# The wide product of a low-rank FFN: two parts in reduced fp32, or plain fp32 on two 64-row tiles

## The chip, the cores and the metric

The kernel runs on one core of a Trainium2 chip. The metric is the device time of one execution in microseconds (us); lower is better. The core has a matrix engine (TensorE, PE in the profile; its weight loads are PEld), VectorE (DVE), ScalarE (ACT), GpSimd (POOL) and SyncE (SP), which issues the DMAs. All of them run their own instruction lists and meet at semaphores.

## The reference

Two layers of a gated cross-attention block over x of 16 x 256 tokens x 256 features: a depooling attention and a coupled FFN (layer 0), then an 8-head cross attention and a low-rank FFN (layer 1). Only the last one is touched:

```python
x = x + tanh(g_ffn[1]) * ffn(layernorm(x))
P = x @ U1                 # 256 -> RANK = 64
H = gelu(P @ V1 + b1)      # 64 -> 1024, the wide product
Q = H @ U2                 # 1024 -> 64
y = Q @ V2 + b2            # 64 -> 256
```

## The kernel before, in words

The 4096 tokens lie in SBUF as 32 tiles of 128 tokens. The kernel goes through stages: A and B (layer 0), C (the attention, one batch `b` of 256 tokens per step, 16 steps) and D (the last FFN, `NG` = 8 groups `n` of 512 tokens). Each engine's order is written out by hand, so an engine that waits holds up everything behind it in its own list; PSUM has eight banks, which are reused by name.

Stage D for one group `n`, with the lines of the profile:

- VectorE normalises four token tiles (`xn_d`, L1788). TensorE transposes them (`xnT_d`, L1351) into banks 4 and 5, ScalarE copies them to `d_xnT` (L910).
- TensorE makes the low-rank product P (`lowrank_d`, L1361). `u1_sb` has 64 columns, and the 512 tokens are cut into two halves of 256: half 0 goes to PSUM partitions 0 to 63 of bank 4, half 1 to partitions 64 to 127. Two feature chunks `c` are summed, so there are four matmuls in plain fp32. VectorE copies each half to `d_pT` as fp32r (L1799: the high part) and writes the rest, value less high part, to the other 64 partitions (L1803: the low part). So `d_pT` holds 64 ranks high and 64 ranks low for all 512 tokens.
- TensorE makes the wide product in four steps `j` of two 128-column tiles `e` (`hidden_d(n, j)`). `v1_sb` holds V1 twice, on partitions 0 to 63 and 64 to 127, and GpSimd has split it once, in stage C, into `v1_hi` and `v1_lo` (`split_v1`, L664 and L666). For each tile a matmul with `v1_hi` (L1439) and one with `v1_lo` (L1440) sum over all 128 rows into one bank: four fp32r matmuls of 512 columns for each `j`.
- ScalarE takes Gelu of two banks (L972) into `d_h`. TensorE makes Q (`second_d(n, j)`, L1449: two column tiles of 64), VectorE copies it (L1870), TensorE makes y (`out_d`, L1462: two row tiles of 64 rows, in banks 7 and 5), VectorE adds it to x (L1877), GpSimd has added b2 before (L680), SyncE stores the group.

The order on TensorE around the change is in `body_d(n)`: hidden 0, hidden 1, transposes of group n+2, second 0, hidden 2, second 1, hidden 3, low-rank product of group n+2, out of group n-1, second 2, second 3. The low-rank products of groups 0 and 1 are made in the last step of stage C (`body_c`), the first two hidden steps of group 0 stand before that stage's last output product (L1325). On VectorE `body_d(n)` is: `xn_d(n + 2)`, `lowrank_d(n + 2)`, `out_d(n - 1)`, `second_d(n)` (the copy of Q).

In the profile a plain fp32 matmul is two records, so "x8" of L1361 is four matmuls; an fp32r matmul is one record. Stage B has one product of the shape used below, `layer4_b` (L1092): weights and data on 64 rows, two tiles `u` on rows 0 to 63 and 64 to 127, 512 columns, plain fp32, banks 0 and 1.

Of the kernel before, what the change touches and what calls it, by code (L numbers as in the profile page):

```python
# [18 lines left out]
F32 = mybir.dt.float32  # L19
F32R = mybir.dt.float32r  # L20
I32 = mybir.dt.int32
BF16 = mybir.dt.bfloat16
ALU = mybir.AluOpType
# [3 lines left out]
P = 128  # L27
# [3 lines left out]
DK = D // P  # L31
FK = DC // P
GROUP = 512
GT = GROUP // P
HALF = GROUP // 2
NG = B * S // GROUP
HEADS, HD = 8, 32
QH = 4
F = 1024
RANK = 64  # L40
# [23 lines left out]
LEAD = 2  # L64
KB = 1024
# [50 lines left out]
def need(eng, sem, count):  # L116

    if isinstance(count, int) and count <= 0:
        return
    eng.wait_ge(sem, count)  # L120
# [22 lines left out]
def beyond(b, n):  # L143
    return isinstance(b, int) and b >= n


def is_last(b, n):
    return isinstance(b, int) and b == n - 1


def is_at(b, n):
    return isinstance(b, int) and b == n


def is_first(b):
    return isinstance(b, int) and b == 0


def build(nc, x, ctx_in, lens, mask, g_xattn, g_ffn, w_in, b_in, g_res, g_init,
# [7 lines left out]
    with ExitStack() as whole:  # L167
        def sb(name, shape, dt=F32, stack=whole):
            return stack.enter_context(nc.sbuf_tensor(name, shape, dt))

        def sem(name):
            return whole.enter_context(nc.semaphore(name))

        banks = whole.enter_context(nc.psum_tensor("bank", [P, 8, 512], F32))
        bank = [banks[:, i, :] for i in range(8)]
# [24 lines left out]
        bk_col = sb("bk_col", [P, DK])  # L200
        bq_col = sb("bq_col", [P, DK])
        neg_row = sb("neg_row", [B, S])
        u1_sb = sb("u1_sb", [P, DK, RANK])
        v1_sb = sb("v1_sb", [P, F // P, P])
        b1_col = sb("b1_col", [P, F // P])
        u2_sb = sb("u2_sb", [P, F // P, RANK])
# [109 lines left out]
            c_sum = [sb(f"c_sum{h}", [P, TS, QH], F32, st) for h in range(2)]  # L316
            c_inv = [sb(f"c_inv{h}", [P, TS, QH], F32, st) for h in range(2)]
        with ExitStack() as st:
            v1_hi = sb("v1_hi", [P, F // P, P], F32R, st)
            v1_lo = sb("v1_lo", [P, F // P, P], F32R, st)  # L320
            d_xn = [sb(f"d_xn{s}", [P, GT, D], F32, st) for s in range(2)]
            d_pT = [sb("d_pT0", [P, GROUP], F32R, st)]
            sb("c_last", [P, 72 * KB // 4], F32, st)
            d_xnT = [sb(f"d_xnT{s}", [P, DK, GROUP], F32, st) for s in range(2)]
            d_h = [sb(f"d_h{s}", [P, 2, GROUP], F32, st) for s in range(2)]
            d_pT += [sb(f"d_pT{s}", [P, GROUP], F32R, st) for s in range(1, LEAD)]
            d_qT = [sb(f"d_qT{s}", [P, HALF], F32, st) for s in range(2)]


        s_lens, s_wa, s_wb, s_wc, s_wd = (sem(n) for n in ("lens_in", "weights_a_in", "weights_b_in",  # L330
                                                           "weights_c_in", "weights_d_in"))
# [28 lines left out]
        b_back, b_x2 = sem("b_result_in_psum"), sem("b_x_updated")  # L360
# [16 lines left out]
        c_nbn, c_nstat, c_npre, c_next = (sem("c_" + n) for n in (  # L377
            "next_bn", "next_moments", "next_chain", "next_stats_ready"))

        s_v1, d_phi = sem("v1_parts_ready"), sem("d_lowrank_high_ready")  # L380
        d_xn_ok, d_xT_ps, d_xT_ok, d_p_ps, d_p_ok, d_h_ps, d_h_ok = (sem("d_" + n) for n in (
            "xn_ready", "xnT_in_psum", "xnT_copied", "lowrank_in_psum", "lowrank_copied",
            "hidden_in_psum", "hidden_ready"))
# [7 lines left out]
        def row_on_all(v):  # L391
# [28 lines left out]
            (arange[:], row_on_all(adaptive_range)),  # L420
        ]
        loads_d = [
            (u1_sb[:], u1.rearrange("(c p) r -> p c r", p=P)),
            (v1_sb[0:RANK], v1.rearrange("r (c f) -> r c f", f=P)),
            (v1_sb[RANK:2 * RANK], v1.rearrange("r (c f) -> r c f", f=P)),
            (b1_col[:], column(b1)), (u2_sb[:], u2.rearrange("(c p) r -> p c r", p=P)),
# [14 lines left out]
        def scores_free(eng, b, hg):  # L441

            n = QH // 2 * (2 * b + hg)
            need(eng, c_pT_act, n)
            need(eng, c_pT_dve, n)
# [83 lines left out]
        def _(pool):  # L529
# [84 lines left out]
            def stats_b(n):  # L614
                next_stats(n, n % 2, GT, b_mv[n % 2], b_tmp[n % 2], b_nstat, b_npre, b_next, n + 1)
# [4 lines left out]
            def bias_c(b):  # L620
                need(pool, c_xn_ok, b + 1)
                xb = x_sb[:, bass.ds(TS * b, TS), :]
                nc.gpsimd.tensor_tensor(xb, xb, bout_b[:].unsqueeze(1).to_broadcast([P, TS, D]),
                                        ALU.add).then_inc(c_xb, 1)
# [9 lines left out]
            def split_q(b):  # L634
                need(pool, c_qhi_ok, b + 1)
                nc.gpsimd.tensor_tensor(c_parts[:, Q_LO, :, :], c_qT[:], c_parts[:, Q_HI, :, :].bitcast(F32),  # L636
                                        ALU.subtract).then_inc(c_qlo_ok, 1)

            def ones_c(s, before, count):
                pool.wait_ge(before, count)  # L640
                nc.gpsimd.memset(c_stack[s][MASK_ROW:MASK_ROW + 1, 0, :, :, :].bitcast(F32), 1.0).then_inc(s_ones, 1)
                pool.wait_ge(s_ones, s + 1)

            def body_c(b, s):
                if not is_last(b, B):
                    split_q(b + 1)
                    bias_c(b + 1)
                if is_first(b):
                    pool.wait_ge(c_xb, 2)
                    ones_c(1, b_x2, NG)  # L650
                if not is_first(b):
                    next_stats(b - 1, 1 - s, TS, n_mv[1 - s], n_tmp[1 - s], c_nstat, c_npre, c_next, b)
                if not beyond(b + 2, B):
                    split_k(b + 2)
                if isinstance(b, int) and b < 2:
                    stats_b(NG // 2 + 2 * b)
                    stats_b(NG // 2 + 2 * b + 1)
                if is_at(b, 1):
                    split_v1()

            def split_v1():
                pool.wait_ge(s_wd, 16 * len(loads_d))
                pool.wait_ge(b_x2, NG)
                nc.gpsimd.tensor_copy(v1_hi[:], v1_sb[:]).then_inc(s_v1, 1)  # L664
                pool.wait_ge(s_v1, 1)
                nc.gpsimd.tensor_tensor(v1_lo[:], v1_sb[:], v1_hi[:].bitcast(F32), ALU.subtract).then_inc(s_v1, 1)  # L666

            split_q(0)
            ones_c(0, c_qlo_ok, 1)
# [320 lines left out]
        def _(pe):  # L990
            mm = nc.tensor.matmul
# [3 lines left out]
            for k in range(TS):  # L995
                op = nc.tensor.transpose(bank[6][:, k * B:(k + 1) * B], bound[:, k * P:(k + 1) * P],
                                         ident[0:B, 0:B])
# [3 lines left out]
            for b in range(B):  # L1001
                for k in range(TS):
                    op = mm(bank[0][0:HI, b * LO:(b + 1) * LO], hit_hi[:, k * B + b, :], hit_lo[:, k * B + b, :],
                            start=k == 0, stop=k == TS - 1)
# [3 lines left out]
            for c in range(DK):  # L1008
                for o in range(DK):
                    op = nc.tensor.transpose(bank[5][:, c * D + o * P:c * D + (o + 1) * P],  # L1010
                                             win_raw[:, o, c * P:(c + 1) * P], ident[:])
# [151 lines left out]
            for lo in range(LO):  # L1163
                op = nc.tensor.transpose(bank[1][0:B, lo:S:LO], ends[:, :, lo], ident[0:HI, 0:HI])
# [190 lines left out]
            def lowrank_d(n):  # L1355
                if n == 0:
                    pe.wait_ge(s_wd, 16 * len(loads_d))
                need(pe, d_xT_ok, 2 * n + 2)
                for c in range(DK):
                    for half in range(2):  # L1360
                        op = mm(bank[4][half * RANK:(half + 1) * RANK, 0:HALF], u1_sb[:, c, :],  # L1361
                                d_xnT[n % 2][:, c, half * HALF:(half + 1) * HALF], start=c == 0, stop=c == DK - 1)
                op.then_inc(d_p_ps, 1)

            def body_c(b, s):
# [31 lines left out]
                if last:  # L1397
                    lowrank_d(1)
# [19 lines left out]
            for k in range(TS):  # L1418
                for f in range(FK):
                    op = mm(bank[3][:, k * D:(k + 1) * D], c_ctxT[0][:, f, k * P:(k + 1) * P],  # L1420
                            wsrcT[:, f, D:2 * D], start=f == 0, stop=f == FK - 1)
# [13 lines left out]
            def hidden_d(n, j):  # L1435
                need(pe, d_p_ok, n + 1)
                need(pe, d_h_ok, 4 * n + j - 1)
                for e in range(2):
                    mm(bank[2 * (j % 2) + e][:], v1_hi[:, 2 * j + e, :], d_pT[n % LEAD][:], start=True, stop=False)  # L1439
                    op = mm(bank[2 * (j % 2) + e][:], v1_lo[:, 2 * j + e, :], d_pT[n % LEAD][:],  # L1440
                            start=False, stop=True)
                op.then_inc(d_h_ps, 1)

            def second_d(n, j):
# [36 lines left out]
                second_d(n, 2)  # L1481
                second_d(n, 3)

            pe.wait_ge(s_v1, 2)
            scores_free(pe, B, 0)
            hidden_d(0, 0)
            hidden_d(0, 1)
# [7 lines left out]
        def _(dve):  # L1495
            v = nc.vector
# [295 lines left out]
            def lowrank_d(n):  # L1792
                need(dve, d_p_ps, n + 1)
                need(dve, d_h_ps, 4 * (n - LEAD + 1))
                parts = [slice(half * RANK, (half + 1) * RANK) for half in range(2)]
                tokens = [slice(half * HALF, (half + 1) * HALF) for half in range(2)]
                pT = d_pT[n % LEAD]
                for half in range(2):
                    op = v.tensor_copy(pT[parts[half], tokens[half]], bank[4][parts[half], 0:HALF])  # L1799
                op.then_inc(d_phi, 1)  # L1800
                need(dve, d_phi, n + 1)
                for half in range(2):
                    op = v.tensor_tensor(pT[parts[1 - half], tokens[half]], bank[4][parts[half], 0:HALF],  # L1803
                                         pT[parts[half], tokens[half]].bitcast(F32), ALU.subtract)
                op.then_inc(d_p_ok, 1)

            def body_c(b, s):
# [110 lines left out]
```

## Time and profile before

| | before |
|---|---|
| median of 3 runs | 746.27 us (742.38, 746.27, 746.42) |
| profiled execution: its own time | 746.62 us |
| profiled execution: span of the trace | 744.8 us |
| PE busy | 687.0 us (92%) |
| DVE, ACT, POOL busy | 513.4, 417.7, 207.5 us |
| stage D with its lead-in, 648 us to the end | 97 us |

The span is what the trace covers; the execution's own time is 1.8 us longer. All times of rows are from the span's start.

### The profile page before, as it was taken

How to read it: one execution, taken by the hardware profiler on the slowest of the kernel's cores; microseconds unless marked ns; L12 is line 12 of the kernel's file. 1: busy time of each engine (PE TensorE's matmuls, PEld its weight loads, DVE VectorE, ACT ScalarE, POOL GpSimd, SP SyncE). 2: the span in 40 equal slices, each digit the busy share in tenths (PEclk: the TensorE clock that was granted, in tenths of full speed). 3: DMA queues.
4: the chain of work that ended last, by engine and by line, in shares of the span. 5: the costliest groups of instructions: out<-in, count | busy, mean ns of one | idle time of the engine just before them, and what ended most of it. 6: DMA issues, size and time to landing. Idle time of an engine off the chain costs nothing.

```text
span 744.8 us, 12430 instructions
## 1 busy us (share of the span) xinstructions
PE 687.0 (92%) x3874; PEld 484.1 (65%) x3874; DVE 513.4 (69%) x976; ACT 417.7 (56%) x1119; POOL 207.5 (28%) x278
## 2 busy tenths in 40 slices
PE   2959999999999999698999999999999997999996
PEld 1646555554544458586888888888888886656553
DVE  6675477755766458879878778878778888735422
ACT  3666645536555534474755665665666567555452
POOL 5454433310110032146132223313232321052110
PEclk9979999999999999799999999999999999999999
DMA  7821103910000004431344432344433223001012
GB/s 199 258 85 57 57 29 105 237 60 1 1 0 1 0 1 113 114 89 50 92 114 113 113 75 73 80 111 113 113 88 87 77 60 86 1 1 57 29 57 86
DMA packets 45752, 57.46 MB, mean 77 GB/s; under 512 B 13808, under 2 KB 24208, under 8 KB 45584
## 3 DMA queue, kind: packets, MB, share of 16 engines
q1 hardware_dynamic: 45712, 56.97, 28.5%
q8 instruction: 20, 0.33, 0.2%
q14 instruction: 20, 0.16, 0.1%
HBM read 27.46 MB, written 4.19 MB: 42 GB/s over the span
## 4 chain that ended last, share of the span: by engine, by line
PE 73%; ACT 9%; DVE 8%; issue 3%; SPq 3%; DMA 2%; POOL 1%; ACTq 0%; DVEq 0%; POOLq 0%
PE bank L1066 11%; PE bank L1325 7%; ACT c_p L882 7%; PE bank L1252 6%; PE bank L1304 6%; PE bank L1078 5%; PE bank L1449 4%; PE bank L1318 4%; PE bank L1291 4%; PE bank L1270 4%; PE bank L1042 4%; DVE c_nmx L1754 3%; PE bank L1046 3%; PE bank L1439 2%; SPq L500 2%
## 5 line engine op out<-in xcount | busy, mean ns | idle before, releaser
L882 ACT ACTIVATE c_p<-bank,c_nmx 128x256 f32<-128x256 f32 x256 | 117.5, 488 | 34.9 <-DVE c_nmx L1754 34.9
L1767 DVE TENSOR_TENSOR c_p<-c_p,c_inv 128x1024 f32<-128x1024 f32 x64 | 90.1, 1409 | 1.1
L1066 PE MATMUL bank<-b_o,cw 128*128 128x512 f32 x192 | 90.8, 603 | 0.0
L1754 DVE TENSOR_REDUCE c_nmx<-bank 128x4 f32<-128x1024 f32 x64 | 75.4, 1219 | 19.1 <-PE bank L1291 19.1
L1304 PE MATMUL bank<-ident,c_p 128*128 128x128 f32 x512 | 66.9, 280 | 13.1 <-ACT c_p L882 13.1
L1304 PEld LDWEIGHTS bank<-ident,c_p 128*128 128x128 f32 x512 | 59.2, 144 | 21.6 <-ACT c_p L882 12.3
L738 ACT ACTIVATE b_h<-bank,cb 128x512 f32<-128x512 f32 x48 | 33.0, 687 | 55.9 <-PE bank L1066 55.9
L1252 PE MATMUL bank<-c_ctxT,wsrcT 128*128 128x256 f32 x256 | 62.2, 388 | 1.4 <-ACT c_ctxT L858 1.4
L972 ACT ACTIVATE d_h<-bank,b_col 128x512 f32<-128x512 f32 x64 | 39.6, 686 | 39.6 <-PE bank L1440 39.6
L1066 PEld LDWEIGHTS bank<-b_o,cw 128*128 128x128 f32 x192 | 34.2, 190 | 41.6 <-issue 41.2
L1774 DVE COPY c_pT<-bank 128x512 f32<-128x512 f32 x64 | 44.0, 687 | 21.7 <-PE bank L1304 21.7
L1270 PE MATMUL bank<-wsrcT,c_ctxT 128*128 128x256 f32 x240 | 56.7, 379 | 0.0
L882 ACT ACTIVATION_READ_ACCUMULATOR c_p<-bank,c_nmx 128x1 f32 x256 | 56.3, 220 | 0.0
L636 POOL TENSOR_TENSOR c_parts<-c_qT,c_parts 128x512 fp32r<-128x512 f32 x16 | 20.6, 1290 | 124.9 <-ACT c_parts L864 124.9
L1252 PEld LDWEIGHTS bank<-c_ctxT,wsrcT 128*128 128x128 f32 x256 | 48.4, 194 | 8.1 <-ACT c_ctxT L858 1.9
L1270 PEld LDWEIGHTS bank<-wsrcT,c_ctxT 128*128 128x128 f32 x240 | 45.5, 190 | 6.2
L892 ACT COPY c_pT<-bank 128x512 f32<-128x512 f32 x64 | 38.0, 599 | 11.1 <-PE bank L1304 11.1
L1629 DVE TENSOR_SCALAR b_tt<-b_tt,k_tt,b_kb 128x256 f32<-128x256 f32 x48 | 17.7, 410 | 37.6 <-ACT b_tt L754 37.6
L1078 PE MATMUL bank<-b_h,cw 128*128 128x512 f32 x96 | 43.3, 592 | 0.0
L1291 PEld LDWEIGHTS bank<-c_stack 97*128 97x128 f32 x256 | 32.8, 191 | 15.7 <-issue 12.1
L1291 PE MATMUL bank<-c_stack 97*128 97x256 f32 x256 | 39.5, 298 | 3.0 <-DMA c_stack<-neg_row 3.0
L897 ACT COPY c_upT<-bank 128x256 f32<-128x256 f32 x32 | 11.9, 373 | 53.9 <-PE bank L1318 53.9
(188 smaller groups left out, 1390.2 us busy)
## 6 DMA issues: line engine op xcount, KB each, us to landing
c_stack<-c_parts SPq DMA_DIRECT2D x192, 128.0 KB
a_ctx<-in_ctx SPq DMA_DIRECT2D x16, 512.0 KB, 3.6
c_ctx<-in_ctx SPq DMA_DIRECT2D x16, 512.0 KB, 3.4
out_x<-x_sb SPq DMA_DIRECT2D x8, 512.0 KB, 3.0
x_sb<-in_x SPq DMA_DIRECT2D x3, 1024.0 KB, 9.9
mask_b<-in_mask_BxS_fk SPq DMA_DIRECT2D x1, 2048.0 KB, 12.4
x_sb<-in_x SPq DMA_DIRECT2D x2, 512.0 KB, 7.5
wsrc_raw<-in_L_xattn_W_src SPq DMA_DIRECT2D x1, 1024.0 KB, 6.9
```

What stands on the lines that cost most here:

```text
L882: op = nc.scalar.activation(c_p[hg][:, tc, j, :], scores(tc)[:, j, :], ACT.Exp, bias=c_nmx[hg][:, tc, j:j + 1], accum_out=c_sum[hg][:, tc, ...
L972: op = nc.scalar.activation(d_h[j % 2][:, e, :], bank[2 * (j % 2) + e][:], ACT.Gelu_apprx_tanh, bias=b1_col[:, 2 * j + e:2 * j + e + 1])
L1066: op = mm(bank[2 * u + h][:], cw1[:, c, h * P:(h + 1) * P], b_o[n % LANES][:, c, :], start=c == 0, stop=c == DK - 1)
L1078: op = mm(bank[4 + u][:], cw2[:, c, :], b_h1[u][:, c, :], start=i == 0, stop=i == DK - 1)
L1252: op = mm(bank[dst][:, m * S:(m + 1) * S], wsrcT[:, f, m * P:(m + 1) * P], c_ctxT[s][:, f, :], start=f == 0, stop=f == FK - 1)
L1270: op = mm(bank[4][:, k * D:(k + 1) * D], c_ctxT[s][:, f, k * P:(k + 1) * P], wsrcT[:, f, D:2 * D], start=f == 0, stop=f == FK - 1)
L1291: op = mm(scores(tc)[:, j, :], c_stack[s][:, 0, j, hg, tc * P:(tc + 1) * P], c_stack[s][:, 1, j, hg, :], start=True, stop=True)
L1304: op = nc.tensor.transpose(bank[j][:, q * S + tc * P:q * S + (tc + 1) * P], c_p[hg][:, tc, j, q * P:(q + 1) * P], ident[:])
L1325: return mm(bank[7][:, k * D:(k + 1) * D], src[:, k * P:(k + 1) * P], woutT[:, f, :], start=f == 0, stop=f == 2 * DK - 1)
L1754: v.tensor_reduce(c_nmx[hg][:, tc, :], scores(tc), AXIS.X, ALU.max, negate=True)\
L1767: v.tensor_tensor(pr, pr, c_inv[hg][:, :, js].unsqueeze(3).to_broadcast([P, TS, 2, S]), ALU.mult)\
L1774: v.tensor_copy(c_pT[hg][:, j, :], bank[j][:]).then_inc(c_pT_dve, 1)
```

## The change

V1 is no longer split: the wide product takes `v1_sb` and P as they are, in plain fp32. For that P has to stand on partitions 0 to 63 and again on 64 to 127, for all 512 tokens. This is done in the low-rank product: `u1_sb` holds U1 twice side by side (128 columns, one more load), and two matmuls of 512 tokens and 128 columns take the place of four of 256 tokens and 64 columns. VectorE then makes one copy of the whole bank. In `hidden_d` tile e = 0 is computed on rows 0 to 63 and tile e = 1 on rows 64 to 127, each with one fp32 matmul. `split_v1` and both semaphores of the parts go; a placeholder keeps the memory of what follows in its place.

```diff
-        u1_sb = sb("u1_sb", [P, DK, RANK])
+        u1_sb = sb("u1_sb", [P, DK, 2 * RANK])
...
-            v1_hi = sb("v1_hi", [P, F // P, P], F32R, st)
-            v1_lo = sb("v1_lo", [P, F // P, P], F32R, st)
+            sb("b_last", [P, 8 * KB // 4], F32, st)
-            d_pT = [sb("d_pT0", [P, GROUP], F32R, st)]
+            d_pT = [sb("d_pT0", [P, GROUP], F32, st)]
...
-            (u1_sb[:], u1.rearrange("(c p) r -> p c r", p=P)),
+            (u1_sb[:, :, 0:RANK], u1.rearrange("(c p) r -> p c r", p=P)),
+            (u1_sb[:, :, RANK:2 * RANK], u1.rearrange("(c p) r -> p c r", p=P)),
...
-                if is_at(b, 1):
-                    split_v1()
...
                 for c in range(DK):
-                    for half in range(2):
-                        op = mm(bank[4][half * RANK:(half + 1) * RANK, 0:HALF], u1_sb[:, c, :],
-                                d_xnT[n % 2][:, c, half * HALF:(half + 1) * HALF], start=c == 0, stop=c == DK - 1)
+                    op = mm(bank[4][:], u1_sb[:, c, :], d_xnT[n % 2][:, c, :], start=c == 0, stop=c == DK - 1)
                 op.then_inc(d_p_ps, 1)
...
                 for e in range(2):
-                    mm(bank[2 * (j % 2) + e][:], v1_hi[:, 2 * j + e, :], d_pT[n % LEAD][:], start=True, stop=False)
-                    op = mm(bank[2 * (j % 2) + e][:], v1_lo[:, 2 * j + e, :], d_pT[n % LEAD][:],
-                            start=False, stop=True)
+                    rows = slice(e * RANK, (e + 1) * RANK)
+                    op = mm(bank[2 * (j % 2) + e][:], v1_sb[rows, 2 * j + e, :], d_pT[n % LEAD][rows, :],
+                            start=True, stop=True)
                 op.then_inc(d_h_ps, 1)
...
-            pe.wait_ge(s_v1, 2)
             scores_free(pe, B, 0)
...
             def lowrank_d(n):
                 need(dve, d_p_ps, n + 1)
                 need(dve, d_h_ps, 4 * (n - LEAD + 1))
-                parts = [slice(half * RANK, (half + 1) * RANK) for half in range(2)]
-                tokens = [slice(half * HALF, (half + 1) * HALF) for half in range(2)]
-                pT = d_pT[n % LEAD]
-                for half in range(2):
-                    op = v.tensor_copy(pT[parts[half], tokens[half]], bank[4][parts[half], 0:HALF])
-                op.then_inc(d_phi, 1)
-                need(dve, d_phi, n + 1)
-                for half in range(2):
-                    op = v.tensor_tensor(pT[parts[1 - half], tokens[half]], bank[4][parts[half], 0:HALF],
-                                         pT[parts[half], tokens[half]].bitcast(F32), ALU.subtract)
+                op = v.tensor_copy(d_pT[n % LEAD][:], bank[4][:])
                 op.then_inc(d_p_ok, 1)
```

## Rows read from the trace of the kernel before

**Rows 1.** The page: busy time of each engine; shares of the chain that ended last.

```profile
PE 687.0 (92%) x3874; PEld 484.1 (65%) x3874; DVE 513.4 (69%) x976; ACT 417.7 (56%) x1119; POOL 207.5 (28%) x278
...
PE 73%; ACT 9%; DVE 8%; issue 3%; SPq 3%; DMA 2%; POOL 1%; ACTq 0%; DVEq 0%; POOLq 0%
```

**Rows 2.** Timeline (start, length, engine, line, count), PE, one group of stage D.

```profile
695.81 0.50 PE L1439 MATMUL bank<-d_pT,v_hi 128*128 128x512 f32 x1
...
697.86 1.09 PE L1351 MATMUL bank<-ident,d_xn 128*128 128x128 f32 x8
698.88 1.08 PE L1449 MATMUL bank<-d_h,u_sb 128*64 128x256 f32 x8
699.90 0.50 PE L1439 MATMUL bank<-d_pT,v_hi 128*128 128x512 f32 x1
...
701.03 1.08 PE L1449 MATMUL bank<-d_h,u_sb 128*64 128x256 f32 x8
...
703.17 1.08 PE L1361 MATMUL bank<-d_xnT,u_sb 128*64 128x256 f32 x8
...
704.18 1.14 PE L1462 MATMUL bank<-v_sb,d_qT 64*128 64x256 f32 x8
...
705.25 1.95 PE L1449 MATMUL bank<-d_h,u_sb 128*64 128x256 f32 x16
...
707.13 0.50 PE L1439 MATMUL bank<-d_pT,v_hi 128*128 128x512 f32 x1
```

**Rows 3.** Timeline, DVE, the same group.

```profile
696.10 0.41 DVE L1870 COPY d_qT<-bank 128x256 f32<-128x256 f32 x1
...
696.43 1.38 DVE L1788 TENSOR_SCALAR d_xn<-x_sb,mu,rstd 128x256 f32<-128x256 f32 x4
...
704.30 0.86 DVE L1799 CAST d_pT<-bank 64x256 fp32r<-64x256 f32 x2 [6.50 <-PE bank L1361]
```

**Rows 4.** Timeline, PE, stage B around one row-tiled product in plain fp32.

```profile
96.59 1.13 PE L1092 MATMUL bank<-b_h,cw 64*128 64x512 f32 x4
...
97.65 1.98 PE L1066 MATMUL bank<-b_o,cw 128*128 128x512 f32 x4
...
99.47 0.60 PE L1029 MATMUL bank<-ident,a_xs 128*128 128x128 f32 x4
```

**Rows 5.** Timeline of PE from 277.60 to 277.75 us: what is under way then.

```profile
277.69 0.70 PE L1092 MATMUL bank<-b_h,cw 64*128 64x512 f32 x2
```

**Rows 6.** Windows: us, busy PE, PEld, DVE, ACT, POOL (x), PE clock, DMA, GB/s.

```profile
718.43:728.22 9.79, 9.36 (x59) 5.48 (x57) 2.10 (x4) 4.96 (x8) 0.00 (x0) 1.00 0.16 54
```

**Rows 7.** Timeline, last step of stage C.

```profile
629.44 1.06 PE L1304 MATMUL bank<-ident,c_p 128*128 128x128 f32 x8 [1.63 <-ACT c_p L882]
...
638.30 1.08 PE L1361 MATMUL bank<-d_xnT,u_sb 128*64 128x256 f32 x8
...
640.44 0.69 DVE L1774 COPY c_pT<-bank 128x512 f32<-128x512 f32 x1 [0.22 <-PE bank L1304]
...
643.21 1.07 PE L1318 MATMUL bank<-c_pT,c_v 128*32 128x256 f32 x16 [1.57 <-issue]
```

**Rows 8.** Timeline, groups 0 and 1 of stage D.

```profile
655.66 7.09 POOL L680 TENSOR_TENSOR x_sb<-x_sb,b_b 128x1024 f32<-128x1024 f32 x3
...
661.16 2.72 DVE L1788 TENSOR_SCALAR d_xn<-x_sb,mu,rstd 128x256 f32<-128x256 f32 x4
...
663.93 1.09 PE L1351 MATMUL bank<-ident,d_xn 128*128 128x128 f32 x8 [1.29 <-DVE d_xn L1788]
```

**Rows 9.** Timeline, PE, group 6: the product behind its first Gelu.

```profile
720.99 1.08 PE L1449 MATMUL bank<-d_h,u_sb 128*64 128x256 f32 x8 [0.43 <-ACT d_h L972]
```

**Rows 10.** Timeline, stage C, batch 2: the split of V1 and what stands beside it.

```profile
344.07 2.36 POOL L666 TENSOR_TENSOR v_lo<-v_sb,v_hi 128x1024 fp32r<-128x1024 f32 x1
...
344.66 2.24 DVE L1727 TENSOR_SCALAR c_xn<-x_sb,mu,rstd 128x256 f32 x2
...
346.76 1.97 PE L1304 MATMUL bank<-ident,c_p 128*128 128x128 f32 x8 [0.57 <-ACT c_p L882]
```

More of the change, by code:

```diff
@@ L325, in build @@
             d_h = [sb(f"d_h{s}", [P, 2, GROUP], F32, st) for s in range(2)]
-            d_pT += [sb(f"d_pT{s}", [P, GROUP], F32R, st) for s in range(1, LEAD)]
+            d_pT += [sb(f"d_pT{s}", [P, GROUP], F32, st) for s in range(1, LEAD)]
             d_qT = [sb(f"d_qT{s}", [P, HALF], F32, st) for s in range(2)]
@@ L378, in build @@
             "next_bn", "next_moments", "next_chain", "next_stats_ready"))
-        s_v1, d_phi = sem("v1_parts_ready"), sem("d_lowrank_high_ready")
         d_xn_ok, d_xT_ps, d_xT_ok, d_p_ps, d_p_ok, d_h_ps, d_h_ok = (sem("d_" + n) for n in (
@@ L657, in body_c @@
                     stats_b(NG // 2 + 2 * b + 1)
-                if is_at(b, 1):
-                    split_v1()
[L661 to L666, printed above, removed]
             split_q(0)
```

## The prediction

> **What bounds the kernel now.** The page first: PE is busy 92% of the span and holds 73% of the chain that ended last [rows 1]. An average says nothing of the last stage, so the timeline of one of its groups comes next [rows 2]: from 695.81 to 707.13 us, 11.32 us for group 3, PE goes from product to product with no gap over 0.1 us. Stage D is bound by PE's own list. Two places are not: the transposes of a later group may wait for VectorE (below), and in groups 6 and 7, which have no transposes to fill in, PE waits for Gelu [rows 9]; such a group takes 9.79 us with PE busy for 9.36, at the full granted clock, 1.00, which is 2.4 GHz [rows 6].
>
> **Streaming and switches.** An isolated hidden step, four fp32r records, takes 1.13 us to the next product (699.90 to 701.03), two steps in a row 2.05 (695.81 to 697.86) [rows 2]. So four further records cost 0.92, 0.23 each, and 0.21 goes at the borders. Those borders are changes of the tile shape: after one, four plain fp32 records of 128 rows and 512 columns take 1.82 us (97.65 to 99.47) [rows 4]; a plain fp32 record of that size is twice one fp32r record less overhead, about 0.43, four are 1.72, and 0.10 is the tail of the switch. The rest of the 0.21 stands ahead of the first record.
>
> **Part 1, the wide product.** The new step is two matmuls on 64 rows, 512 columns, plain fp32: four records. This very form is in stage B: L1092 takes 1.06 us from its start to the next product (96.59 to 97.65) [rows 4], with two records under way at once [rows 5]; in a row they would need 4 x 0.43 = 1.72. So an isolated step goes from 1.13 to 1.06, a gain of 0.07, not the half that the count of matmuls (16 to 8 for each group) suggests. The pair in a row goes from 2.05 to 1.06 + 0.86 = 1.92, and then comes a switch to the transposes that was not there, 0.10 ahead of them and 0.10 after their first record.
> The Trainium skill, "TensorEngine Tiling (Array Packing)", Key Properties, speaks against the change here: going to another tiling mode, not just another tile, drains the engine. The trace agrees with its 0.2 us for each switch. By that rule alone each of six groups pays 0.2 more, in full.
> By the rows part of it is covered. From 695.81 to 697.86 VectorE also runs a chain: it copies Q at 696.10, normalises from 696.43 for 1.38 to 697.81, and the transposes start 0.05 later [rows 2, 3]. The chain starts when Q's last product is out, and the change leaves it alone, so the transposes start 2.05 after the hidden step as before. I charge only the 0.10 after their first record, between 0 (the switch is done while PE waits) and 0.20.
>
> **Part 2, the low-rank product.** Now 1.01 us to the next product (703.17 to 704.18) [rows 2], two column tiles at a time. After: four records of 128 x 128, 512 columns, behind a switch, 1.82 [rows 4], and 0.09 to the row-tiled out product, 1.91: +0.90 for each of groups 0 to 5. In group 0 no out product stands between it and second 2; a switch more, +0.10.
> For low-rank product 1, at the end of stage C, both neighbours are 128 x 128, so it takes 1.72 and starts 0.10 earlier than at 638.30: the next product is 0.61 later. Is that on the path? VectorE waited for that next product, 0.22 us, at 640.44, and the work behind its copy releases the product at 643.21 [rows 7]. So yes: +0.61, bounds 0 and 0.90. Low-rank product 0 costs nothing: behind it PE waits 1.63 us for ScalarE's exponentials [rows 7]; without that cover it would be 0.9 too.
>
> **Part 3, VectorE.** Four operations of 64 x 256, two in 0.86 us [rows 3] and as much again for the two subtractions, give way to one 128 x 512 copy from PSUM, 0.69 [rows 7]: 1.1 us less for each group. It is worth nothing in steady groups: P for group n+2 is used a group later. Behind it on VectorE stand `out_d`, the copy of Q and the normalising. The copy begins 0.9 later than now, ends 0.2 earlier, and two additions follow before second 3 is out; none of this is late.
>
> **Part 4, GpSimd and the load.** The split goes: 2.36 us for the low part [rows 10] and less for the high one. Beside it VectorE's two normalisings take 2.24 us where four take 1.38 [rows 3, 10]. But PE's next transposes at 346.76 are released by ScalarE's exponentials, not by VectorE [rows 10]: I take 0; bounds: a gain up to 1.5, a loss of 0. The second load of U1 is one issue more on SP, ahead of its wait for the end of stage A; SP's next loads stand behind that wait, and U1 is used only at the end of stage C. I take 0; without that cover it is the length of one issue, well under 1 us.
>
> **The sum, from the first shift on.**
> - End of stage C: +0.61. Group 0: hidden 0 and 1 +0.07 (a switch more before the output product), hidden 2 and 3 -0.14, low-rank +1.00: +0.93. Together +1.54.
> - Group 1's transposes at 663.93 waited 1.29 us for VectorE. Its normalising took 2.72 where 1.38 is usual, from 661.16 on; three GpSimd operations ran until 655.66 + 7.09 = 662.75 [rows 3, 8]. It looks as if the first of the four had to wait for GpSimd; from 662.75 to its end are 1.14. GpSimd comes only 0.68 later (0.61 + 0.07), VectorE could start 1.54 later, at 662.70, still before 663.43: the transposes come 0.68 later. The wait swallows the rest; what is left is +0.68. Bounds: 0.1 and the full 1.6.
> - Rest of group 1: -0.14 + 0.90 = +0.76. Groups 2 to 5: 4 x 0.76 = +3.04. The tail of the new switch in groups 1 to 5: 5 x 0.10 = +0.50.
> - Groups 6 and 7: no low-rank product; three pieces of hidden work on the path, 2 x 3 x -0.07 = -0.42 (the wait for Gelu stays, and starts a little earlier).
> Sum: 0.68 + 0.76 + 3.04 + 0.50 - 0.42 = +4.56 us. The span goes to 749.4, the profiled execution's own time from 746.62 to 751.2. That execution is 0.35 above the median of the runs, 746.27, so the median becomes 750.8, 0.6% more. With all low bounds the sum is 2.0 (3.5, less 1.5 from stage C), with all high ones 6.3 (another 0.3 from stage C, 0.92 without the wait, 0.5 of switches).
>
> **The rivals.**
> - The row tiles do not overlap (slower). Place: every hidden step; each takes 1.72 + 0.2 in place of 1.06, or 0.86 more, 32 steps: +27.5, 778 us. It decides as soon as a tenth of it comes true. For it: weights of both tiles come from one tensor. Against: L1092 is the same form and overlaps [rows 4, 5]. 0.03.
> - A new wait (slower). VectorE has a cushion of some 0.6 us between its second addition and the copy of Q; if the later low-rank copy eats it, the copy of Q, the normalising and the transposes slide. Each microsecond per group is 5 us; at 0.7 per group the time is 754.5. For it: 2.05 was already VectorE's chain. Against: the new copy is shorter. 0.08.
> - The gains elsewhere cancel the loss (same). If taking the split away frees the attention step of batch 2, and group 1's wait takes all, 747 us. 0.09.
> - The wide product halves (faster): if the two tiles ran with records as short as fp32r's 0.23, a step would take 0.67, 0.4 less in 32 steps: 738 us. Against: L1092's 1.06. 0.02. The Trainium skill, "TensorEngine Tiling (Array Packing)", Theoretical Speedup, gives up to twofold for a contraction of 64; the trace shows that, but against plain fp32, not against the fp32r records of now.
> - The forecast, 0.78: a loss of 2.0 to 6.3 us.
>
> **The numbers.** Predicted 750.8. One of the three runs before was 3.9 below the others, so a median may fall low: the range is 746.5 to 754.5, and leaves out what lies beyond the bounds and the first and last rival. What a measurement of this kernel can tell from no change is 1%, 7.5 us: below 738.8 or above 753.7. Faster 0.02; slower 0.10 (the serial tiles, most of the new wait); same 0.88.
>
> **What the profile after would show.** Hidden steps of 1.06 us alone and transposes 2.05 after a pair's start: right; 1.7 or more: serial tiles. The low-rank product 1.9 us to the next. A steady group of about 12.2 in place of 11.32 us. Group 1's transposes near 664.6. Stage C before 638 unmoved; a shift there is what I have priced at nothing. If the transposes are released by VectorE more than 2.1 after the pair's start, it is the new wait.

## The result and the profile after

| | before | after |
|---|---|---|
| median | 746.01 us (742.38 to 748.39, 13 runs) | 748.69 us (747.08 to 750.99, 13 runs) |
| ratio, with 95% interval | | 1.0041 [1.0025, 1.0057] |
| profiled execution: its span | 744.8 us | 746.8 us |
| PE / DVE / ACT / POOL busy | 687.0 / 513.4 / 417.7 / 207.5 us | 687.5 / 505.3 / 417.5 / 204.1 us |

By the ratio the change costs 3.1 us (1.9 to 4.3); the two medians lie 2.7 apart. That is within the 1% that I called no change, clear of zero, and the time is inside the range of 746.5 to 754.5. 750.8 was predicted, 2.1 too much. The engines' busy times say where not to look: VectorE and GpSimd work less than before [rows 1], and the kernel is slower all the same.

The start of an execution scatters: the kernel after, e3, e4 and e5 have the same instructions up to stage D, and they reach the first product of attention probabilities and values of stage C (L1308) between 307.5 and 310.5 us. From 352 us on, the two traces keep their distance through all of stage C (the same product comes at 351.95 before and 351.16 after, and the transposes of its last step at 629.44 and 628.65, both times 0.79 earlier). So I compare stretches from the end of stage C on. First a steady group after, in the timeline of PE (start, length, engine, line, count); the wide product is now L1428, the low-rank product L1350, the transposes L1341, second L1437, out L1450:

```profile
697.59 1.99 PE L1428 MATMUL bank<-d_pT,v_sb 64*128 64x512 f32 x8
...
699.50 1.09 PE L1341 MATMUL bank<-ident,d_xn 128*128 128x128 f32 x8
700.53 1.08 PE L1437 MATMUL bank<-d_h,u_sb 128*64 128x256 f32 x8
...
701.54 1.13 PE L1428 MATMUL bank<-d_pT,v_sb 64*128 64x512 f32 x4
702.60 1.08 PE L1437 MATMUL bank<-d_h,u_sb 128*64 128x256 f32 x8
...
703.61 1.13 PE L1428 MATMUL bank<-d_pT,v_sb 64*128 64x512 f32 x4
704.67 1.98 PE L1350 MATMUL bank<-d_xnT,u_sb 128*128 128x512 f32 x4
...
706.59 1.13 PE L1450 MATMUL bank<-v_sb,d_qT 64*128 64x256 f32 x8
...
707.65 1.95 PE L1437 MATMUL bank<-d_h,u_sb 128*64 128x256 f32 x16
...
709.53 1.99 PE L1428 MATMUL bank<-d_pT,v_sb 64*128 64x512 f32 x8
```

Read it from start to start, against [rows 2]. The group takes 11.94 us instead of 11.32. A hidden step alone takes 1.06 to 1.07 (701.54 to 702.60), not 1.13. The low-rank product takes 1.92 (704.67 to 706.59), not 1.01. And the two hidden steps in a row take 1.91 to the transposes (697.59 to 699.50), where the prediction kept the 2.05 of before. The reason is on VectorE, in the same stretch:

```profile
697.70 0.42 DVE L1848 COPY d_qT<-bank 128x256 f32<-128x256 f32 x1 [0.47 <-PE bank L1437]
...
698.04 1.37 DVE L1775 TENSOR_SCALAR d_xn<-x_sb,mu,rstd 128x256 f32<-128x256 f32 x4
...
706.70 0.69 DVE L1782 COPY d_pT<-bank 128x512 f32<-128x512 f32 x1 [7.28 <-PE bank L1350]
...
707.77 1.41 DVE L1855 SCALAR_TENSOR_TENSOR x_sb<-bank,gates,x_sb 128x512 f32<-128x512 f32 x2 [0.38 <-PE bank L1450]
```

The copy of Q starts 0.11 us behind the hidden step's start and has waited for PE. Before, it started 0.29 behind (696.10 against 695.81) [rows 2, 3], without any wait: VectorE still had its additions to finish, which had stood behind four low-rank operations. The additions of that group in the timeline before:

```profile
694.77 1.41 DVE L1877 SCALAR_TENSOR_TENSOR x_sb<-bank,gates,x_sb 128x512 f32<-128x512 f32 x2
696.10 0.41 DVE L1870 COPY d_qT<-bank 128x256 f32<-128x256 f32 x1
```

Where the first extra time arises, and how much of it group 1's wait takes back (timeline after: low-rank product 1 on PE, VectorE's copy of c_pT behind it, the product that waits for that copy's successors, then PE and VectorE in group 1):

```profile
637.42 1.88 PE L1350 MATMUL bank<-d_xnT,u_sb 128*128 128x512 f32 x4
...
640.21 0.69 DVE L1761 COPY c_pT<-bank 128x512 f32<-128x512 f32 x1 [0.77 <-PE bank L1294]
...
642.97 1.07 PE L1308 MATMUL bank<-c_pT,c_v 128*32 128x256 f32 x16 [1.93 <-issue]
...
661.28 1.99 PE L1428 MATMUL bank<-d_pT,v_sb 64*128 64x512 f32 x8
...
661.74 1.88 DVE L1775 TENSOR_SCALAR d_xn<-x_sb,mu,rstd 128x256 f32<-128x256 f32 x4
...
663.68 1.09 PE L1341 MATMUL bank<-ident,d_xn 128*128 128x128 f32 x8 [0.40 <-DVE d_xn L1775]
```

VectorE now waits 0.77 us for PE at the end of stage C where it waited 0.22 [rows 7]: 0.55 more, straight onto the path. PE waits 0.40 us for VectorE in group 1 where it waited 1.29 [rows 8].

The books of the two traces, each stretch from a product's start to another's, in us. "Update product" is the product of attention probabilities and values (L1318 before, L1308 after), the last one before stage D; "tail" is the prediction's charge for the new switch:

| stretch | before | after | difference | predicted |
|---|---|---|---|---|
| end of stage C: 629.44 to 643.21; 628.65 to 642.97 | 13.77 | 14.32 | +0.55 | +0.61 |
| group 0: last update product to group 1's first hidden step | 13.52 | 14.51 | +0.99 | +0.93 |
| group 1: that step to its transposes | 3.40 | 2.40 | -1.00 | -0.86 |
| rest of group 1 | 9.27 | 10.02 | +0.75 | +0.76, +0.10 tail |
| groups 2 to 5 | 45.23 | 47.77 | +2.54 | +3.04, +0.40 tails |
| groups 6 and 7, to the last out product | 20.16 | 19.37 | -0.79 | -0.42 |
| sum | | | +3.04 | +4.56 |

The sum of the stretches, 3.04, agrees with the 3.1 of the timed runs. It is 1.52 under the predicted sum, and the misses hardly cancel: 0.90 of the 1.52 lies in groups 2 to 5, 0.37 in groups 6 and 7.

### The profile page after: what moved, and what is told of

It is laid out like the page before. It is cut to its first block, busy times and chain, and to the rows that moved or that the text cites. A ratio compares the mean times of both kernels' runs of the same rounds, so it can differ in the third digit from the quotient of the medians.

```text
span 746.8 us, 12339 instructions
## 1 busy us (share of the span) xinstructions
PE 687.5 (92%) x3842; PEld 471.2 (63%) x3842; DVE 505.3 (68%) x952; ACT 417.5 (56%) x1119; POOL 204.1 (27%) x276
## 4 chain that ended last, share of the span: by engine, by line
PE 73%; DVE 9%; ACT 9%; issue 3%; SPq 3%; DMA 2%; POOL 1%; ACTq 0%; DVEq 0%; POOLq 0%
PE bank L1056 11%; PE bank L1315 7%; ACT c_p L872 6%; PE bank L1242 6%; PE bank L1294 6%; PE bank L1068 5%; PE bank L1437 4%; PE bank L1308 4%; PE bank L1428 4%; PE bank L1260 4%; PE bank L1281 4%; PE bank L1032 3%; DVE c_nmx L1741 3%; PE bank L1036 2%; SPq L499 2%
## 5 line engine op out<-in xcount | busy, mean ns | idle before, releaser
L1294 PE MATMUL bank<-ident,c_p 128*128 128x128 f32 x512 | 65.4, 277 | 12.7 <-ACT c_p L872 12.7
```

What stands on the lines that cost most here:

```text
L1294: op = nc.tensor.transpose(bank[j][:, q * S + tc * P:q * S + (tc + 1) * P], c_p[hg][:, tc, j, q * P:(q + 1) * P], ident[:])
```

## The experiments

Theory A, from the prediction and the traces: the doubled low-rank product is the whole loss; the wide product, at the same rate as before, gives a little back; what VectorE has in its list ahead of its copy of Q also counts. Each of the rivals is in the texts below. Times of kernels are against the kernel before in the same runs, whose median was 745.5 us for the first four and 745.4 for the last four.

### One part alone: the doubled low-rank product (e1)

```diff
 # before.py with the doubled u1_sb and its two matmuls, and in VectorE's lowrank_d:
+                pT, low = d_pT[n % LEAD], slice(RANK, 2 * RANK)
+                v.tensor_copy(pT[:], bank[4][:]).then_inc(d_phi, 1)
+                need(dve, d_phi, n + 1)
+                op = v.tensor_tensor(pT[low, :], bank[4][low, :], pT[low, :].bitcast(F32), ALU.subtract)
```

> Only the low-rank product is doubled (128 columns, 512 tokens); the wide product stays on the high and low parts in fp32r, VectorE makes one 128x512 copy and one 64x512 subtraction. Theory A (the whole loss is the doubled low-rank product, the wide product gives a little back): low-rank product to the out product 1.8 us instead of 1.01, a steady group 11.9 to 12.0 us instead of 11.32, the time about 3.5 to 4 us over the kernel before, that is at least as much as with the full change. Rival B (the loss is the wide product in plain fp32, with its changes of tile shape): most of the loss is gone, within 1 us of the kernel before.

Measured: 748.56 us, ratio 1.0040 [1.0024, 1.0055], the same as with the full change; that is 3.0 us over the kernel before, a little less than the 3.5 to 4 expected. In the timeline of PE, the ends of one steady group and its low-rank product (L1361; L1461 is out):

```profile
697.63 0.50 PE L1438 MATMUL bank<-d_pT,v_hi 128*128 128x512 f32 x1
...
699.58 1.04 PE L1352 MATMUL bank<-ident,d_xn 128*128 128x128 f32 x8
700.55 1.08 PE L1448 MATMUL bank<-d_h,u_sb 128*64 128x256 f32 x8
...
704.74 1.88 PE L1361 MATMUL bank<-d_xnT,u_sb 128*128 128x512 f32 x4
...
706.55 1.14 PE L1461 MATMUL bank<-v_sb,d_qT 64*128 64x256 f32 x8
...
709.49 0.50 PE L1438 MATMUL bank<-d_pT,v_hi 128*128 128x512 f32 x1
```

1.81 us for the low-rank product and 11.86 for the group. The loss of the full change is there without its wide product; rival B falls. The lines show one thing more: the hidden steps are those of before, but VectorE has two operations of P instead of four, and the pair takes 1.95 to the transposes (L1352) instead of 2.05, these 0.97 to second 0 instead of 1.02.

### The other part alone: the wide product (e2)

```diff
 # after.py with u1_sb, its load and lowrank_d of TensorE as before; VectorE:
-                op = v.tensor_copy(d_pT[n % LEAD][:], bank[4][:])
+                for half in range(2):
+                    src = slice(half * RANK, (half + 1) * RANK)
+                    for dst in (src, slice((1 - half) * RANK, (2 - half) * RANK)):
+                        op = v.tensor_copy(d_pT[n % LEAD][dst, half * HALF:(half + 1) * HALF], bank[4][src, 0:HALF])
```

> Only the wide product is changed (plain fp32 on two 64-row tiles); the low-rank product stays as two column tiles of 64, and VectorE makes four 64x256 copies so that P stands on both halves of the partitions. Theory A: hidden steps 1.06 us, the pair to the transposes 2.05 because VectorE still has four operations ahead of its chain, a steady group 11.19 us, groups 6 and 7 about 9.4 instead of 9.79; 1.5 us under the kernel before. Rival B: slower than the kernel before by 2 to 3 us. Rival C (VectorE's queue does not matter, TensorE alone sets the group): the pair to the transposes is 1.92 here too, a steady group 11.05.

Measured: 743.20 us, ratio 0.9976 [0.9964, 0.9988]: by the ratio 1.8 us faster than before (0.9 to 2.7). Timeline, PE and VectorE, one group:

```profile
694.40 1.99 PE L1429 MATMUL bank<-d_pT,v_sb 64*128 64x512 f32 x8
694.67 0.41 DVE L1852 COPY d_qT<-bank 128x256 f32<-128x256 f32 x1
...
696.43 1.09 PE L1340 MATMUL bank<-ident,d_xn 128*128 128x128 f32 x8
...
702.73 1.73 DVE L1786 COPY d_pT<-bank 64x256 f32<-64x256 f32 x4 [6.36 <-PE bank L1350]
...
705.55 1.99 PE L1429 MATMUL bank<-d_pT,v_sb 64*128 64x512 f32 x8
```

The group takes 11.15 us. The pair to the transposes takes 2.03, although the hidden steps are those of the changed kernel: with four operations back in VectorE's list the copy of Q starts 0.27 late again. Rival C, under which it would be 1.92, falls.

### No second row tile (e3)

```diff
-                    rows = slice(e * RANK, (e + 1) * RANK)
+                    rows = slice(0, RANK)
```

> The changed kernel with both 128-column tiles of a hidden step computed on rows 0 to 63, so that no two matmuls stand on different row tiles. Theory A (the two row tiles work at the same time, each record takes 0.43 us): a hidden step takes 1.72 + 0.2 = 1.9 us instead of 1.06, 32 steps, about +27 us, 775 us. Rival D (a record of 64 rows is simply half as long, whatever the tile): a hidden step stays at 1.06, 749 us.

Measured, one execution: 775.62 us, span 772.9. A hidden step in the timeline of PE, and the product behind it:

```profile
701.43 1.98 PE L1428 MATMUL bank<-d_pT,v_sb 64*128 64x512 f32 x4
703.34 1.08 PE L1437 MATMUL bank<-d_h,u_sb 128*64 128x256 f32 x8
```

1.91 us in place of 1.06. So a plain fp32 record of 512 columns takes 0.43 us on 64 rows as on 128 (1.91 less 0.2 at the borders, by four), rival D falls, and the 1.06 comes from two of them at a time. This is the price of the first rival of the prediction, had it come true: 27 us.

### More work on VectorE (e4)

```diff
                 op = v.tensor_copy(d_pT[n % LEAD][:], bank[4][:])
+                for i in range(4):
+                    rows = slice(i % 2 * RANK, (i % 2 + 1) * RANK)
+                    op = v.tensor_copy(d_junk[rows, i * HALF:(i + 1) * HALF], bank[4][rows, 0:HALF])
```

> The changed kernel with four more 64x256 copies (4 x 0.43 = 1.72 us) on VectorE behind the copy of P, into memory that nothing reads. Theory A (VectorE's list has some 0.85 us to spare between the copy of P and the copy of Q; what goes over it is paid in the wait of the transposes): the pair of hidden steps to the transposes 2.75 to 2.8 us instead of 1.91, a steady group 12.8 instead of 11.94, 752 us. The step as the prediction put it (VectorE's operations here are worth nothing in steady groups): 11.94, 749 us.

Measured, one execution: 750.19 us, 2 under the 752 expected. Timeline of one group:

```profile
697.67 1.99 PE L1428 MATMUL bank<-d_pT,v_sb 64*128 64x512 f32 x8
698.52 0.41 DVE L1851 COPY d_qT<-bank 128x256 f32<-128x256 f32 x1
...
700.28 1.09 PE L1341 MATMUL bank<-ident,d_xn 128*128 128x128 f32 x8 [0.62 <-DVE d_xn L1775]
...
710.30 1.99 PE L1428 MATMUL bank<-d_pT,v_sb 64*128 64x512 f32 x8
```

A group of 12.63 us, the pair to the transposes 2.61: 0.70 more for 1.72 more work, so 1.0 us of VectorE's work is free here, not the 0.85 of theory A. Groups 2 to 5 make 2.8 us of it in the trace; the single execution shows 1.5 over the median of the kernel after, within the scatter of the start. That VectorE's work is worth nothing is refuted by the transposes' wait, not by the whole time.

### GpSimd out of VectorE's way (e5)

```diff
-            def bias_d(n, s):
-                need(pool, d_xn_ok, n + 1)
+            def bias_d(n):
+                need(pool, d_xn_ok, n + 2 if n == LEAD else n + 1)
...
-            over_pairs(pool, NG, bias_d)
+            for n in range(NG):
+                bias_d(n)
```

> The changed kernel; GpSimd's bias addition for group 2 waits until VectorE has normalised group 3, so GpSimd is idle while VectorE normalises group 3. Theory A (the wait of group 1's transposes is VectorE's first normalising operation held up by GpSimd's running addition): the four operations take 1.38 us instead of 1.88, the transposes come about 1.92 us after the pair of hidden steps' start, set by TensorE's own list, instead of 2.40; half a microsecond less, 748.2 us. Rival (it is the copy of Q or the semaphores' latency that make them late): 2.40 stays.

Measured, one execution: 747.79 us; 748.2 was expected, and a single time cannot tell it from the 748.7 of the kernel after. Timeline, groups 0 and 1:

```profile
655.11 4.67 POOL L670 TENSOR_TENSOR x_sb<-x_sb,b_b 128x1024 f32<-128x1024 f32 x2
...
660.89 1.99 PE L1429 MATMUL bank<-d_pT,v_sb 64*128 64x512 f32 x8
...
661.35 1.37 DVE L1776 TENSOR_SCALAR d_xn<-x_sb,mu,rstd 128x256 f32<-128x256 f32 x4
...
662.81 1.09 PE L1342 MATMUL bank<-ident,d_xn 128*128 128x128 f32 x8
```

With GpSimd idle the four operations take 1.37 us instead of 1.88, and the transposes come 1.92 behind the pair's start instead of 2.40. The wait in group 1, which swallowed a microsecond of the change's cost, was GpSimd's addition in front of VectorE; the rival, by which 2.40 stays, falls.

### Toward a faster kernel (e6, e7, e8)

e6 is e2 with the four copies moved to ScalarE, behind its last Gelu of a group:

```diff
 # ScalarE, for n >= LEAD; VectorE's lowrank_d returns there
+            def lowrank_d(n):
+                need(act, d_p_ps, n + 1)
+                need(act, d_h_ps, 4 * (n - LEAD + 1))
+                (the four copies of e2, with nc.scalar.copy)
+                op.then_inc(d_p_ok, 1)
```

> As e2 (only the wide product changed, the low-rank product in two column tiles of 64), but for groups 2 to 7 ScalarE makes the four copies of P, after its last Gelu of the group, and VectorE makes none. Theory A (in e2 VectorE's four copies push its copy of Q back by 0.15 us): the pair to the transposes 1.92 us instead of 2.03, a steady group 11.03 instead of 11.15, ScalarE still done with the copies before its next Gelu; some 0.5 us under e2, 742.7 us. Rival E (ScalarE's queue becomes the wait): the next Gelu starts late and a steady group is 11.3 or more.

e7 adds the diff of e5:

> e6 with the later bias addition of e5. Theory A: group 1's transposes, which in e2 came 3.43 us after the pair's start, come 2.0 to 2.1 us after it; 1.4 us under e6, 741.3 us, 0.6% under the kernel before. Rival: the wait stays, because another operation of VectorE is late.

e8 is e7 with, in `body_d` of TensorE:

```diff
+                if n + LEAD < NG:
+                    need(pe, d_xT_ok, 2 * (n + LEAD) + 2)
+                if n > 0:
+                    out_d(n - 1, 1 - n % 2)
                 if n + LEAD < NG:
                     lowrank_d(n + LEAD)
-                if n > 0:
-                    out_d(n - 1, 1 - n % 2)
```

> e7 with the out product of the group before moved ahead of the low-rank product, so that it follows the hidden step in the same tile shape (64 rows) and the low-rank product stands beside second 2 in the same shape (64 columns). Theory A (0.1 us ahead of and 0.1 behind each change of tile shape, which these two moves save): hidden 3 to out 0.96 us, out to low-rank product 1.06, low-rank product to second 2 0.92; a steady group 10.85 us, five groups, about 1 us under e7, 740.4 us. Rival (the shape costs nothing, the 0.2 is the latency of a semaphore wait at the head of each product): as e7.

| kernel | time | ratio to before, 95% interval | steady group | stage D |
|---|---|---|---|---|
| before | 745.4 to 746.0 | 1 | 11.32 | 91.6 |
| after | 748.69 | 1.0041 [1.0025, 1.0057] | 11.94 | 94.1 |
| e2 | 743.20 | 0.9976 [0.9964, 0.9988] | 11.15 | 90.0 |
| e6 | 744.57 | 0.9991 [0.9974, 1.0008] | 11.04 | 89.6 |
| e7 | 742.39 | 0.9966 [0.9950, 0.9981] | 11.04 | 88.2 |
| e8 | 741.71 | 0.9948 [0.9928, 0.9968] | 10.69 | 86.4 |

"Stage D" is the distance in the trace from the last update product of stage C to the last out product. By it e6 is 0.44 us under e2, as expected, and e7 1.4 under e6. The whole times of e6 do not show it: 742.7 was expected, and its median is 1.4 over e2's, with an interval that holds 1. The profiled execution of e6 loses its time before stage D, which it enters 2.5 us later than e2's (below). In e7 group 1's transposes come 2.02 us behind the pair's start, where e2 has 3.43. Rival E falls too: ScalarE's four copies take 1.49 us and it is idle for 2.37 behind them.

e8 gained more than expected in a group, 0.35 instead of 0.2. Its timeline of PE:

```profile
707.84 1.13 PE L1441 MATMUL bank<-d_pT,v_sb 64*128 64x512 f32 x4
708.90 1.08 PE L1450 MATMUL bank<-d_h,u_sb 128*64 128x256 f32 x8
709.91 1.13 PE L1441 MATMUL bank<-d_pT,v_sb 64*128 64x512 f32 x4
710.88 1.03 PE L1463 MATMUL bank<-v_sb,d_qT 64*128 64x256 f32 x8
711.84 1.08 PE L1362 MATMUL bank<-d_xnT,u_sb 128*64 128x256 f32 x8
712.75 1.90 PE L1450 MATMUL bank<-d_h,u_sb 128*64 128x256 f32 x16
714.58 1.99 PE L1441 MATMUL bank<-d_pT,v_sb 64*128 64x512 f32 x8
```

The same hidden step costs 1.06 us before a product of another shape (707.84) and 0.97 before out, which has its own shape (709.91). Out costs 0.96 instead of 1.07, the low-rank product 0.91 instead of 1.01. The rival, a wait's latency at each product's head, would have left them as they were; e8 even has a wait more ahead of out. It has the lowest median of the kernels run, by the ratio 3.9 us under the one before (2.4 to 5.4). It is not shown to be faster than e7: the two intervals overlap, the medians are 0.7 apart where stage D says 1.8, and e8's profiled execution enters stage D 2.1 us later than e7's. Both stayed above what was expected, 741.3 for e7 and 740.4 for e8.

## Why the prediction was right, and where it was off

**The wide product** was right: 1.06 us alone, because the trace of before had the very form. Halving the matmuls was never worth half the time: one fp32r record is 0.23 us, one plain fp32 record 0.43, and the two row tiles just make up for the difference (e3).

**The low-rank product** was right, and it is the loss: 1.92 us measured, 1.91 predicted. e1 has the whole loss, e2 has none of it. Low-rank product 0, in the gap of stage C, was free, as said: PE still waits behind it, 1.19 us instead of 1.63 [rows 7].

**The end of stage C** was right in place and size, +0.55 against +0.61.

**"It is worth nothing in steady groups" was wrong.** The prediction saw that VectorE's chain to the transposes set 2.05 us, but let it start "when Q's last product is out", and gave VectorE "a cushion of some 0.6 us" ahead of the copy of Q. The trace of before has no such cushion: the additions run until 696.18, and the copy starts at 696.10. It started 0.29 us after the hidden step instead of 0.11, since it stood behind the additions, and those behind four low-rank operations. One copy in place of four operations takes VectorE off the path, and the transposes come 0.14 us earlier in each group: 0.6 us over groups 2 to 5. e2 brings 2.03 back, e4 takes it to 2.61. In e1, with the hidden steps of before, the pair takes 1.95: so 0.10 of the 2.05 was VectorE's, which the prediction had read as a border. The sign that it gave for itself, transposes 2.05 after a pair's start, did not come.

**The tail of the new switch** was charged at 0.10 us in five groups, as an addition to 1.02; transposes to second 0 is 1.03 us after and 1.02 before [rows 2], and nothing was added. Both halves of the term were off. The tail is about 0.05 here: 0.97 in e1, where the transposes follow in the same shape and VectorE does not hold them up, and 1.02 in e3, where they follow 64-row matmuls and VectorE has been ready for 1.8 us. And the 1.02 of before already held 0.05 more than e1's 0.97, beside the wait for VectorE. Why a wait costs as much as a switch there is not shown. The Trainium skill, "TensorEngine Tiling (Array Packing)", Key Properties, says that a change of mode drains the engine. The trace agrees where larger products follow without a gap, as e8 shows with 0.1 us at either side.

**Group 1's wait** was right in kind. GpSimd's running addition held up VectorE (e5 shows it), and its slack swallowed 1.00 us (predicted 0.86).

**Groups 6 and 7** gained 0.79 us, not 0.42. The term missed something that the order shows: with no low-rank product between them, hidden 3 and out now have the same shape, which saves a switch. A window of group 6 after, to hold against [rows 6] (us, then busy PE, PEld, DVE, ACT, POOL, clock, DMA, GB/s):

```profile
721.47:730.86 9.39, 8.88 (x59) 4.10 (x57) 1.83 (x3) 4.96 (x8) 0.00 (x0) 1.00 0.17 56
```

9.79 became 9.39: three times 0.07 and two borders of 0.1. PE's wait for Gelu stays, 0.51 us after and 0.43 before [rows 9].

**The split of V1** was rightly priced at nothing. Without it VectorE's two normalisings take 0.73 us instead of 2.24 [rows 10], but PE's transposes wait for the exponentials as before, and the two products of that step lie 1.83 us apart in both traces. Timeline after:

```profile
343.40 0.73 DVE L1714 TENSOR_SCALAR c_xn<-x_sb,mu,rstd 128x256 f32 x2
...
345.50 1.97 PE L1294 MATMUL bank<-ident,c_p 128*128 128x128 f32 x8 [0.74 <-ACT c_p L872]
```

## What to carry to other kernels

When an engine's list is full, count every product's time at its own shape and precision from a row, and the borders between shapes as products of their own: here the operation that feeds the change cost more than the change gained. Ask of a shorter operation on a second engine not only who needs its result, but what stands behind it in that engine's list. And if two parts can be had apart, try them apart: the wide product alone is a little faster than before (0.2%), the doubled low-rank product alone is all of the loss.

## What the runs showed of the hardware that I had not expected

A fall of TensorE's clock in the last steps of stage C, in some executions only. Windows of e8 (same columns as above):

```profile
620.00:630.00 10.00, 6.86 (x60) 5.00 (x60) 9.45 (x19) 6.99 (x25) 1.04 (x3) 1.00 0.21 48
630.00:640.00 10.00, 9.64 (x61) 7.52 (x62) 6.86 (x9) 5.50 (x20) 0.00 (x0) 0.83 0.01 2
```

After a stretch in which PE was busy for 6.86 of 10 us, the mean granted clock was 0.83 over the next 10, that is, part of them at the lower level of 1.2 GHz. In the kernel before PE was busy for 7.18 us of the same stretch and the clock stayed at 1.00:

```profile
620.00:630.00 10.00, 7.18 (x65) 5.29 (x64) 9.84 (x20) 6.99 (x25) 1.04 (x3) 1.00 0.29 66
630.00:640.00 10.00, 9.24 (x71) 6.94 (x70) 7.85 (x12) 6.86 (x26) 0.00 (x0) 1.00 0.01 2
```

e6's profiled execution fell as well, at the same code, to 0.83, and there PE had been busy for 7.19 us; in e2 and e7 it had been busy for 6.89 and 6.99, and the clock stayed at 1.00. So the busy time of the 10 us before does not tell the two cases apart. The end of stage C (the first stretch of the table of books) takes 15.23 us in e8 and 15.27 in e6, against 13.77 before: 1.5 us, as much as most steps of this case. The same two executions lost time once before: from 345 to 355 us the mean granted clock was 0.69 in e6 and 0.75 in e8, but 0.83 before, 0.84 in e2 and 0.87 in e7, and the step of stage C there took 17.3 us in both against 15.5 to 15.6 in those three. Whether e6 and e8 fall more often than the others is open: one profiled execution of each cannot tell, and the whole times of the kernel before scatter over 5 us too. That such falls are why e6's median hides the gain of its stage D is likely, but not shown.

The other surprise is how completely VectorE's normalising stood still beside GpSimd: the first operation that met a running addition did not run slower, it waited for the addition's end, and those behind it took their usual time. The first one of group 1 before, its three followers having 0.40 us each, and GpSimd's additions ending at 662.75 [rows 8]:

```profile
661.16 1.75 DVE L1788 TENSOR_SCALAR d_xn<-x_sb,mu,rstd 128x256 f32<-128x256 f32 x1
```

Two normalisings took 2.24 us beside the split and 0.73 without it; four took 2.72 before and 1.37 in e5. It does not hold for all of VectorE's work: its copies out of PSUM ran beside the same additions in their usual time, the copy of Q in group 0 in 0.42 us at 660.70.
